# A two-layer graph network on one core: layer 1's bin coding and ranking moved from ahead of the gathers to beside layer 0's first 176 gathers

## The reference

```python
# layer 0: sums over dst of the rows of src
x_l = x @ W_l.T + b_l
agg = segment_sum(x_l[src], dst);  deg = segment_sum(1, dst)
x = layernorm(x + agg / max(deg, 1) + x @ W_r.T)
# layer 1: sums over src of the rows of dst
neigh = segment_sum(x[dst] @ W_neigh.T + b_neigh, src) / max(deg, 1)
out = relu(x @ W_self.T + b_self + neigh)
x = layernorm(x + layernorm(x + out) * gamma + beta)
```

## Time and profile before

| | us |
|---|---|
| median of 3 runs | 3032.01 (3031.95 to 3041.6) |
| the profiled execution, its own time | 3039.64 |
| its span, first to last instruction | 3037.9 |
| PE, DVE, ACT, POOL busy | 2376.5, 1960.0, 1421.2, 1998.1 |
| prologue, up to the first one-hot of layer 0 | 0 to 155.4 |
| layer 0's stream, up to its last add | 155.4 to 1357.3 |

### The profile page before, as it was taken

How to read it: one execution, slowest core, us unless ns; L and a number is a source line. 1 busy time by engine, 2 the same in 40 slices (tenths; PEclk the granted TensorE clock), 3 DMA queues, 4 the chain that set the end, 5 groups by cost and what they waited for, 6 DMA issues and landing times.

```text
span 3037.9 us, 52213 instructions
## 1 busy us (share of the span) xinstructions
PE 2376.5 (78%) x10032; PEld 1021.4 (34%) x10032; DVE 1960.0 (65%) x4549; ACT 1421.2 (47%) x3617; POOL 1998.1 (66%) x2069
## 2 busy tenths in 40 slices
PE   3288989989999988987885677776767777666996
PEld 2133434444444434433432232222323222221443
DVE  6899888888888888877873333333333333322898
ACT  3502555555565555553444443444344433431676
POOL 0276777777777777761115777777777777774785
PEclk8589999999999999999997989899888899865998
DMA  5577777777788777774557888888888888778676
GB/s 197 174 198 229 230 221 232 222 234 233 227 234 232 228 229 234 219 208 125 166 166 232 250 250 251 252 245 248 247 246 250 250 246 251 224 204 153 226 241 203
DMA packets 250848, 676.72 MB, mean 223 GB/s; under 512 B 40360, under 2 KB 41190, under 8 KB 250788
## 3 DMA queue, kind: packets, MB, share of 16 engines
q0 software_dynamic: 148480, 488.56, 57.0%
q1 hardware_dynamic: 101828, 186.19, 18.3%
q10 hardware_dynamic: 480, 1.28, 0.1%
HBM read 585.90 MB, written 89.97 MB: 222 GB/s over the span
## 4 chain that ended last, share of the span: by engine, by line
PE 32%; DMA 26%; DVE 17%; issue 14%; POOL 6%; DVEq 3%; ACT 1%; POOLq 1%; SPq 0%; ACTq 0%
PE ps L1117 31%; DMA rows<-table,idx_ring 13%; DMA flat<-table,idx_ring 9%; POOL rows L541 3%; DVE acc L889 2%; DVE onehot L876 2%; DVEq L883 2%; DMA table<-rows 1%; DVE where L901 1%; DMA edges<-table,idx_ring 1%; POOL flat L541 1%; POOL rows L525 1%; DVE flat L1072 1%; DVE spot L1072 1%; DVE flat L1089 1%
## 5 line engine op out<-in xcount | busy, mean ns | idle before, releaser
L1117 PE MATMUL ps<-rows,onehot 128*128 128x512 f16 x4176 | 895.3, 332 | 348.0 <-DMA rows<-table,idx_ring 172.3
L525 POOL DMA_INDIRECT rows<-table,idx_ring x928 | 895.1, 965 | 313.5 <-issue 207.5
L961 DVE TENSOR_TENSOR acc<-acc,ps 128x513 f32 x464 | 320.1, 690 | 798.2 <-PE ps L1117 795.5
L1117 PEld LDWEIGHTS ps<-rows,onehot 128*128 128x128 bf16 x4176 | 374.7, 102 | 919.3 <-issue 194.7
L541 POOL DMA_INDIRECT rows<-table,idx_ring x464 | 438.5, 945 | 158.5 <-issue 99.9
L1117 PE MATMUL ps<-where,put 128*128 128x464 bf16 x1664 | 467.9, 363 | 36.7 <-DVE where L901 28.2
L1117 PE MATMUL ps<-w_b,flat 128*128 128x512 f32 x784 | 463.4, 675 | 0.0
L901 DVE TENSOR_SCALAR where<-iota_chunk,cw_ring 128x928 bf16<-128x928 f16 x832 | 438.0, 526 | 7.5 <-PE ps L1117 0.6
L1425 ACT ACTIVATE put<-spot,flat 128x128 f16<-128x128 f16 x832 | 265.7, 390 | 338.1 <-PE ps L1117 330.7
L1413 ACT ACTIVATE spot<-iota_node,flat 128x128 f16<-128x128 f16 x832 | 340.4, 479 | 128.4 <-DVE flat L745 128.4
L889 DVE TENSOR_TENSOR acc<-acc,ps 128x513 f32 x464 | 318.1, 686 | 95.3 <-PE ps L1117 49.8
(11 more groups left out here) (233 smaller groups left out, 2450.2 us busy)
## 6 DMA issues: line engine op xcount, KB each, us to landing
table<-rows SPq DMA_DIRECT2D x98, 257.0 KB, 4.0
rows<-table,idx_ring POOLq DMA_INDIRECT x1392, 3.8
xr_scratch<-edges SPq DMA_DIRECT2D x49, 256.0 KB
rows<-xr_scratch SPq DMA_DIRECT2D x49, 256.0 KB, 3.2
h_scratch<-rows SPq DMA_DIRECT2D x49, 256.0 KB, 2.1
flat<-h_scratch SPq DMA_DIRECT2D x49, 256.0 KB
hb_scratch<-spot SPq DMA_DIRECT2D x49, 256.0 KB, 3.8
u_scratch<-flat SPq DMA_DIRECT2D x49, 256.0 KB
```

The source lines that it names most:

```text
L525: nc.gpsimd.indirect_dma_start(out=rows[:, k % GB, :], out_offset=None, in_=tables[layer][:, :], in_offset=bass.IndirectOffsetOnAxis(ap=id ...
L961: V.tensor_tensor(tile_acc, tile_acc, part, ALU.add).then_inc(s_acc, 1)
L1117: return nc.tensor.matmul(*args, skip_group_check=True, **kw)
```

## The change

Three things are changed, each in the stage ahead of or beside layer 0's stream.

1. **Listing.** All of layer 1's coding, counting and ranking leaves the prologue. On DVE it becomes a generator, `listing()`, and on PE another, `listed()`. Each gives up the engine at every `yield`, and one step is taken of each ahead of every chunk of the first LISTING = 11 iterations (176 chunks). The counts now go to banks 0 and 1.
2. **Table.** x is loaded in seven batches of seven tiles, and each batch's maxima, scales, `high`, `low`, tails and stores follow as it arrives. ACT now finds the maxima of six batches, DVE those of the last.
3. **Placing.** PC = 18 columns per iteration in 46 iterations (BODIES = 23 pairs), and 4 in the last, which also carries the products of the last four tiles and three turns. A third `put` buffer is added.

```diff
-        RANKING = CHUNKS[0] // U - EC // U
-        RIDE = U // GROUP[0]
-        AHEAD = T - RANKING * RIDE
+        PC = 18
+        BODIES = (EC - 1) // (2 * PC)
+        LAST_COLS = EC - 2 * BODIES * PC
+        LISTING = CHUNKS[0] // U - 2 * BODIES - 1
...
-            bin_starts(1)
...
-            for b in range(AHEAD):
-                bin_rank(1, b)
-            for t in range(T):
-                low(t)
             hand_over(0, 0, 0)
+            lows(2)
+            scales(4)
+            lows(3)
+            scales(5)
+            lows(4)
+            scales(6)
+            lows(5)
+            lows(6)
...
+            def listing():
...
+                for b in range(T):
+                    make_mask(s, b, b)
+                    if b % 2 == 1:
+                        yield
...
+                for b in range(T):
+                    dve.wait_ge(s["used"], T + b + 1)
+                    if b:
+                        dve.wait_ge(s["max"], b)
+                    at = 2 * (b % RB[1])
+                    V.tensor_tensor(pos.rearrange(halves, h=2), pos.rearrange(halves, h=2), ps[:, at:at + 2, 0:HC],
+                                    ALU.max).then_inc(s["max"], 1)
+                    yield
+                    if b + MB < T:
+                        make_mask(s, T + b + MB, b + MB)
+                    yield
...
+                    if lister is not None:
+                        next(lister, None)
                     if place is not None:
-                        spread(place, k, isinstance(place, int) and place == 0)
+                        for j in range(k * cols // U, (k + 1) * cols // U):
+                            spread(place, j, half, isinstance(place, int) and place == 0)
                     hot(layer, i, k, first and layer == 0)
-                    if rank and k % g == g - 1:
-                        bin_rank(1, AHEAD + RIDE * i + k // g)
...
+            def listed():
...
+                for b in range(T):
+                    rank_bin(1, b)
+                    yield
+                    yield
...
                 for k in range(U):
+                    if lister is not None:
+                        next(lister, None)
                     if placing is not None:
-                        place(1, U * placing + k, k, start=(isinstance(placing, int) and placing == 0 and k == 0),
-                              stop=(isinstance(placing, int) and placing == EC // U - 1 and k == U - 1))
-                    if rank and k % g == 0:
-                        rank_bin(1, AHEAD + RIDE * i + k // g)
+                        for j in range(k * cols // U, (k + 1) * cols // U):
+                            place(1, PC * placing + j, PC * half + j, put_at=(PC * half + j) // PB % 3,
+                                  start=(isinstance(placing, int) and placing == 0 and j == 0), stop=(last and j == cols - 1))
...
+                    if last and k % 4 == 0:
+                        for j in range(KC):
+                            x_product(T - 4 + k // 4, j)
+                    if last and k % 4 == 2 and k < 12:
+                        x_turn(T - 3 + k // 4, (T - 3 + k // 4) % 2)
...
+            def bounds(b):
+                act.wait_ge(s_x[b], 16)
+                for t in range(BATCH * b, BATCH * b + BATCH):
...
+                    nc.scalar.activation(spot[:, 4 * (t % 2):4 * (t % 2) + 4, :].rearrange("p a c -> p (a c)"), acc[:, t, 0:D],
+                                         ACT.Abs, accum_out=top[:, t:t + 1]).then_inc(s_bound, 1)
...
+            bounds(0)
+            for b in range(1, DVE_MAXIMA):
+                bounds(b)
+                highs(b - 1)
+            for b in range(DVE_MAXIMA - 1, T // BATCH):
+                highs(b)
```

More of the change, by code:

```diff
@@ L216, in gnn_two_layers @@
         s_vec = sem("s_vec")
-        s_x = [sem(f"s_x{k}") for k in range(5)]
+        s_x = [sem(f"s_x{k}") for k in range(T // BATCH)]
         s_iota = sem("s_iota")
@@ L919, in add_beta, with chunks @@
                 V.tensor_tensor(hbout, hin, vec[4], ALU.add).then_inc(s_lhb, 1)
-            def chunks(layer, i, first=False, last=False, place=None, rank=False, side=None, half=0):
+            def chunks(layer, i, first=False, last=False, place=None, lister=None, side=None, half=0):
                 g = GROUP[layer]
+                cols = LAST_COLS if last else PC
                 for k in range(U):
@@ L941, in chunks @@
                     if side is not None and k == 11:
-                        x_evict(side, half)
+                        x_evict(side, 1 - half)
+                    if last and k % 4 == 3:
+                        x_evict(T - 4 + k // 4, (T - 4 + k // 4) % 2)
                 if last:
@@ L1136, in _, with count_bin, first_chunks, chunk_tiles @@
             last.then_inc(s_win, 1)
-            def prepare(layer):
-                s = lists[layer]
+            def count_bin(layer, b):
+                s, bank = lists[layer], (6, 0)[layer]
+                pe.wait_ge(s["mask"], b + 1)
+                for h in range(2):
+                    last = mm(ps[0:T, bank + h, 0:HC], unit[:, T - 1 - b:2 * T - 1 - b], mask[b % MB][:, h * HC:(h + 1) * HC],
+                              start=(b == 0), stop=(b == T - 1))
+                last.then_inc(s["used"], 1)
+            def first_chunks(layer):
+                s, bank = lists[layer], (6, 2)[layer]
+                pe.wait_ge(s["cs"], 1)
+                mm(ps[0:T, bank, 0:1], tri[0:T, 0:T], nch[:], start=True, stop=True).then_inc(s["cscol"], 1)
+            def chunk_tiles(layer):
+                s, bank = lists[layer], (6, 0)[layer]
+                pe.wait_ge(s["past"], 1)
+                half = GROUPS[layer] // 2
+                for b in range(2):
+                    last = mm(ps[0:1, bank + b, 0:half], past_bins[:, 0:1], past[:, b * half:(b + 1) * half],
+                              start=True, stop=True)
+                last.then_inc(s["tile"], 1)
+            def prepare():
+                s = lists[0]
                 pe.wait_ge(s_mark, 1)
@@ new lines, in puts @@
+            def puts(c, g):
+                s, col, at = lists[1], 2 * PC * c + PB * g, PB * (g % 3)
+                first = isinstance(c, int) and c == 0 and g < 3
+                if not first:
+                    act.wait_ge(s["put"], col - 2 * PB)
+                for k in range(PB):
+                    last = nc.scalar.activation(spot[:, at + k, :], iota_node[:], ACT.Abs,
+                                                scale=value[:, ds(col + k, 1)], bias=shift_v[:, ds(col + k, 1)])
+                last.then_inc(s["spot"], 1)
+                made = PC // 2 * c + g + 1
+                free = col - 2 * PB
+                if not isinstance(made, int):
+                    made, free = act.to_reg(made), act.to_reg(free)
+                act.wait_ge(s_code, 1)
+                act.wait_ge(s["spot"], made)
+                if not first:
+                    act.wait_ge(s["placed"], free)
+                for k in range(PB):
+                    nc.scalar.activation(puts_of[g % 3][:, k, :], spot[:, at + k, :], ACT.Relu, scale=-1.0,
+                                         bias=value[:, ds(col + k, 1)]).then_inc(s["put"], 1)
```

448 lines of the change are left out of this document (253 added, 195 removed).

## The result

The changed kernel takes 3144.44 us (median of 4 runs, 3140.08 to 3146.85) against 3032.91 us (4 runs) of the kernel before: ratio 1.036, interval 1.0336 to 1.0383. It is 111.5 us slower; the prediction had 49 us slower, with 3132 as the upper end of its range. The sign and the mechanism were right, one term was far too small.

A forecast was written before the change was run, and what follows sets the result against it. POOL's gathers were taken to set the stream's pace. The stream's 311 + 961 + 27 = 1299 us is 97 more than before; less 48 from the prologue, 49 us slower: 3081 us against the median, range 3036 to 3132.

The forecast's parts named there:

- What bounds the kernel: Layer 0's stream: POOL sets the pace, one gather every 1.28 us; DVE has nothing to spare in the ranking.
- the loop: Ranking: `rank_bin`, maximum, one-hot, add, even chunk's sums, next `rank_bin` wait in a ring; 3.80 us per bin at full clock.
- The table: Prologue: table made batch by batch, listing gone; first one-hot at 107 in place of 155.4, 48 us gained.
- The listing, first part: Start of layer 0's stream: masks, coding and counting beside the chunks up to the first maximum, 88 us.
- The ranking: Layer 0's stream: 49 bins at 4.0 us each in a closed loop of PE and DVE, 196 us, bounds 186 and 254.
- The listing, the rest: The 23 chunks left of the eleven listing iterations after the ranking: 27 us, bounds 22 and 32.
- The placing: 46 iterations with two columns more, 20.9 us each: 961 us, bounds 938 and 998.
- The last iteration: End of layer 0's stream: four products, three turns, four columns and sixteen chunks, 27 us, bounds 22 and 35.
- 5.19: Rival, in the ranking: the clock falls to 1.2 GHz, 5.19 us a bin, +58 us, 3139; chance 0.12.
- The sum: Whole kernel: stream 1299 us, 97 more; less 48 from the prologue, 49 us slower, 3081 against the median.
- the ranking keeps its old beat: Rival, in the ranking: the engines slip past each other as before, 2.5 us a bin, sum -24, 3008; chance 0.12.

The follow-up runs named there:

- the filler: The changed kernel with six more matmuls on PE behind each odd chunk of the ranking, their result overwritten by the next `rank_bin`: 3066.43 us, ratio 1.0137.
- experiments 1 and 2: Two variants of the changed kernel: DVE's maximum one chunk later (3010.49 us, ratio 0.9955); PE's `rank_bin` one chunk earlier (3004.06 us, ratio 0.9937).
- experiment 2: The changed kernel with PE's `rank_bin` one chunk earlier, ahead of the even chunk's sums: 3004.06 us, ratio 0.9937; on a third chip 3010.89 us, 0.9949.
- experiment 5: The changed kernel with six more matmuls on PE per ranking pair, in the first ten pairs only: 3547.72 us, ratio 1.0139, on the second chip.
- Experiment 7: The warm kernel: experiment 2's kernel with extra matmuls on PE before the first chunk and each coding chunk: 3466.61 us, 0.9921 (second chip); 3008.27, 0.994 (third).

## Why the prediction was wrong

Its steps, in order, in the profiled execution:

- **What bounds the kernel.** Right. POOL's 1.28 us per gather is the pace of the placing before and after, and in the ranking as soon as the loop is opened.
- **The table.** 48 us predicted, 110.26 for 155.4 is 45.1. ACT had its first tile of x at 19.82 (20 in the working), and ended its last high half at 96.9 (94). Left out was DVE's own clear of 9.04 us from 100.15, behind 2.38 us of idle time. It ends at 109.19 and ACT's four at 109.27, so it cost nothing more.
- **The listing, first part.** 88 predicted, 194.89 - 110.26 = 84.6.
- **The ranking. This is the step that failed.** 49 x 4.0 = 196 predicted, 49 x 5.27 = 258 measured: 62 us. The loop and both of its lengths were right: 3.80 at full clock (3.82 with the filler) and 5.19 at 1.2 GHz (5.27). Wrong was the choice between them. I took the granted clock of 0.86 from layer 1's stream, where PE is busy 72%, laid it on the loop as a mean, and went from the 4.1 that it gave to 4.0; 0.12 was the chance that I gave to 5.19. But the profile held no row of PE in such a loop, and the clock is no mean to interpolate: it sat at one level for all 49 bins. The rule that I had set beside it, in the Trainium skill ("TensorE: Matmul & The Clock Gate", "A second HAM failure mode: psum-queue depth-cycling"), pointed the right way. It speaks of a clock that goes up and down; the trace here differs, with 0.50 throughout and no interval under 5.25. It ties PE's short idle times between groups of matmuls to the cycling through PSUM banks; experiments 1 and 2 keep the cycling and have 0.95 and 0.99 in the ranking, so here the idle times that count come from the wait in the loop.
- **The listing, the rest.** 27 predicted. From the end of the 49th bin, 194.9 + 258.3 = 453.2, to 478.66 it is 25.5.
- **The placing.** 46 x 20.9 = 961 predicted, 46 x 20.60 = 947.6. Two columns more an iteration cost nothing that shows: PE's busy share in 600 to 1000 rose from 92% to 93%, DVE's from 87% to 91%, and POOL kept its beat. My 0.3 us an iteration was a guess between the ends.
- **The last iteration.** 27 predicted, 1426.3 to 1455.7 is 29.4.
- **The sum.** The stream took 1345.4 us for the 1299 predicted: -3.4 + 62.3 - 1.5 - 13.4 + 2.4 = +46.4. With 2.9 less from the prologue the stream ends 49.3 later than predicted. Behind it 4.3 us came on top (102.7 of span for 98.4 at the stream's end), and the rest up to 111.5 is how the two profiled executions stood to their medians.

The rival *the ranking keeps its old beat* was the wrong reading of these queues, but right as a price: its 3008 is what the kernels with the opened loop take (3004 to 3010 where before takes 3024). That the price fits is in part luck: its stream is 1299 - 73 = 1226 us where an opened one takes 1213.5, and the medians show less of the gain than the traces do (below). Less came of it than the 45 us of the prologue because these 1213.5 us (109.64 to 1323.2 in experiment 2) are still more than the 1201.9 of before: the last iteration takes 27.1 for 20.6, and the first 96 gathers, beside the coding, come 1.42 and 1.49 us apart, 17 us more than at 1.28. (The kernel before had a slow start and the stop for `places(1)` in its 1201.9 as well, so these don't add up to the difference.) The stream ends 34, 28 and 25 us earlier than in the trace of before in three profiled executions (experiment 2's kernel twice, the warm one once), and the medians show 20, 15 and 18. The trace of before was taken on another occasion, of an execution 6.7 us above its median; where the rest goes stays open.

## What to carry to other kernels

When work is moved into two in-order queues, write both orders down and look for a ring: an instruction on one engine that stands behind its partner's result, and the partner behind the instruction's. One place forward or back in either queue is enough to open it, and it is worth trying both (here 4.1% and 4.2% of the whole time for a `yield`). When such a ring makes TensorE wait in every turn, price it at 1.2 GHz unless a row of the same kernel shows PE at full clock with waits like those. Here the slower clock made the ring longer (5.27 for 3.82), and the ring brought the clock down again in the first turn without filler.

## What the runs showed of the hardware

- PE was busy 80% of 253 us at a granted clock of 0.50 without a break, and 87% busy at 0.99 in the same loop with the filler. Work that is of no use made the kernel some 68 us faster.
- In experiment 5 the interval of the maxima goes from 3.80 to 5.14 in the first turn without filler, behind one wait of 1.48 us.
- Chips differ in the gathers. On the second chip the kernel before takes 3497 us, 15 to 16% more than in the three other comparisons. In 600 to 1000 experiment 5's kernel has there 257 gathers in place of 313, of the same length, with more idle time ahead of them:

```profile
L538 POOL DMA_INDIRECT rows<-table,idx_ring x257 | 247.3, 962 | 154.0 <-issue 63.5 <-PE ps L1215 53.4 <-remote 37.1
```

That is 1.56 us per gather for 1.28, and 37.1 us of waits that the profile puts down to no engine or transfer of the core ("remote"); the traces of the other chips have none of them in this group. What it is wasn't tried.
- With these slower gathers even the opened order does not keep the full clock. Experiment 7's kernel has 0.82 in its ranking on the second chip, and intervals of the maxima from 2.1 to 5.9, where the same kernel on the third chip is at 1.00 behind its first intervals:

```profile
199.00:351.00 152.00, 134.50 (x583) 46.37 (x582) 119.82 (x261) 0.00 (x0) 91.01 (x96) 0.82 0.59 164
```
